# First layer's PSUM banks dealt anew: three for turned probabilities, one for all dense pieces

## What is computed

```
h = layernorm(x) * (1 + ca) + sa
x = x + ga * attn(h)          # 16 heads of 16, causal, with ALiBi, softmax over keys, then @ o_w
h = layernorm(x) * (1 + cb) + sb
x = x + gb * ffn(h)           # sigmoid(xr @ Wr) * (relu(xk @ Wk)**2 @ Wv), xr and xk mixed with the token before
```

## Time and profile before

| | us |
|---|---|
| median of 3 runs (lowest to highest) | 3240.66 (3238.57 to 3241.61) |
| the profiled execution | 3246.79 |
| its span, first to last instruction | 3245.0 |
| first layer: first transposes to last addition to x | 42.5 to 747.5 |
| of it slots 1 to 31 with the turns | 82.4 to 672.7 |
| drain behind the last AV | 689 to 747.5 |
| TensorE's mean granted clock over the span | 0.944 of full speed |

### The profile page before, as it was taken

The page is one execution under the profiler, slowest core; times in us unless marked ns, Lnnn a source line. Parts: engine busy times, 40 slices in busy tenths (PEclk is TensorE's granted clock), DMA queues, the critical chain, the costliest instruction groups (busy, mean ns, idle before and its releaser), DMA issues. The chain is left out here.

```text
span 3245.0 us, 52986 instructions
## 1 busy us (share of the span) xinstructions
PE 2931.1 (90%) x20772; PEld 1994.1 (61%) x20772; DVE 1657.6 (51%) x5057; ACT 1369.5 (42%) x2997; POOL 856.0 (26%) x830
## 2 busy tenths in 40 slices
PE   5889899975999999999999999999999688879993
PEld 2566666653575757666666666666565343668882
DVE  2566777644555544444444444455554576541114
ACT  2666666632444444445454535353433211112222
POOL 1001111122333332322323233233332100115554
PEclk8999999997999999999999999999999898669996
DMA  4110011004000000000000000100000000202325
GB/s 134 18 18 18 18 18 18 14 3 160 8 4 9 6 17 28 1 1 1 16 29 1 1 1 12 32 6 6 11 6 6 10 1 1 91 24 79 73 85 176
DMA packets 65135, 93.94 MB, mean 29 GB/s; under 512 B 9931, under 2 KB 52942, under 8 KB 63848
## 3 DMA queue, kind: packets, MB, share of 16 engines
q1 hardware_dynamic: 57208, 74.24, 7.9%
q0 software_dynamic: 7680, 16.32, 2.0%
HBM read 59.31 MB, written 27.36 MB: 27 GB/s over the span
## 5 line engine op out<-in xcount | busy, mean ns | idle before, releaser
L1371 PE MATMUL bank<-h2T,w 128*128 128x512 f32 x1024 | 479.4, 606 | 5.1 <-ACT gT L1309 3.7
L1409 PE MATMUL bank<-w,gT 128*128 128x256 f32 x2048 | 465.9, 381 | 0.0
L1409 PEld LDWEIGHTS bank<-w,gT 128*128 128x128 f32 x2048 | 379.3, 190 | 49.7 <-issue 0.5
L1046 POOL TENSOR_TENSOR prob<-prob,rsum 128x512 f32<-128x512 f32 (+1 forms) x256 | 238.1, 951 | 589.9 <-DVE rsum L1193 589.9
L1371 PEld LDWEIGHTS bank<-h2T,w 128*128 128x128 f32 x1024 | 182.4, 190 | 224.1 <-issue 173.9
L1309 ACT ACTIVATE gT<-bank,vec 128x512 f32<-128x512 f32 x256 | 175.1, 687 | 286.0 <-PE bank L1371 284.6
L633 ACT ACTIVATE y<-y,least 128x128 f32<-128x128 f32 (+3 forms) x512 | 251.9, 554 | 50.3 <-DVE least L520 50.2
L520 DVE CUSTOM_DVE_ANT_0 y<-bank,mask 128x128 f32<-128x128 f32 (+3 forms) x512 | 223.9, 486 | 77.0 <-PE bank L726 75.5
L1199 DVE COPY probT<-bank 128x1024 f32<-128x1024 f32 (+1 forms) x128 | 139.2, 1087 | 227.4 <-PE bank L1425 227.4
L1170 DVE CUSTOM_DVE_ANT_0 prob<-bank,mask 128x256 f32<-128x256 f32 (+1 forms) x512 | 164.3, 387 | 167.3 <-PE bank L1361 167.3
L1281 ACT ACTIVATE prob<-prob,least 128x256 f32<-128x256 f32 (+1 forms) x512 | 239.6, 471 | 15.8 <-DVE least L1170 15.4
(11 more groups left out here) (291 smaller groups left out, 5074.9 us busy)
## 6 DMA issues: line engine op xcount, KB each, us to landing
w<-in_W SPq DMA_DIRECT2D x8, 1024.0 KB, 5.5
expert_parts<-zeros SPq DMA_DIRECT2D x8, 1024.0 KB, 16.0
we<-in_we SPq DMA_DIRECT2D x16, 512.0 KB
rows<-modulation SPq DMA_DIRECT2D x40, 128.0 KB, 3.0
x<-in_x SPq DMA_DIRECT2D x8, 512.0 KB, 9.8
prob<-score SPq DMA_DIRECT2D x64, 64.0 KB, 2.4
probT<-score SPq DMA_DIRECT2D x64, 64.0 KB, 2.4
y<-expert_parts SPq DMA_DIRECT2D x8, 512.0 KB, 8.8
```

What stands on the lines that cost most here:

```text
L1046: nc.gpsimd.tensor_tensor(two, two, rsum[:, at:at + 2].unsqueeze(2).to_broadcast([P, 2, width]), ALU.mult).then_inc(s["probs"], 1)
L1371: ins = nc.tensor.matmul(M[m % 2][:, :], w1[:, k, m * P:(m + 1) * P], h2T[:, k, :], start=(k == 0), stop=(k == KD - 1))
L1409: ins = nc.tensor.matmul(M[i][:, (t % 2) * D:(t % 2 + 1) * D], gT[:, m, t * P:(t + 1) * P], w2[:, m, :], start=(m == 0), stop=(m == MF - 1))
```

## The change

`H` gets a third bank (4, 5, 6), and turn number `at` takes bank at % 3, with one semaphore for each bank; a turn waits until the turn three before it is emptied. `M` is bank 7 alone: a dense piece k waits until piece k-1 is emptied. The two pairs of semaphores of the dense pieces stay and still alternate, only `free` waits for k-1. `values` waits for the last three turns rather than the last two. Nothing is computed in another way, and neither the order of any queue nor the engine of any copy changes.

```diff
         def bank_of(x):
-            return M[ORDER0[x] % 2]
+            return M
...
         def free(eng, x):
-            k = ORDER0[x]
-            if k >= 2:
-                eng.wait_ge(s[("misc_out0", "misc_out1")[k % 2]], k // 2)
+            k = ORDER0[x] - 1
+            if k >= 0:
+                eng.wait_ge(s[("misc_out0", "misc_out1")[k % 2]], k // 2 + 1)
...
         def turned_out(eng, k):
-            eng.wait_ge(s[("pt_out0", "pt_out1")[k % 2]], k // 2 + 1)
+            eng.wait_ge(s[("pt_out0", "pt_out1", "pt_out2")[k % 3]], k // 3 + 1)
...
             copy(probT[:, j:j + nj, FROM[tile]:FROM[tile] + width],
-                 H[at % 2][:, 0:nj * width].rearrange("p (j n) -> p j n", j=nj))\
-                .then_inc(s[("pt_out0", "pt_out1")[at % 2]], 1)
+                 H[at % 3][:, 0:nj * width].rearrange("p (j n) -> p j n", j=nj))\
+                .then_inc(s[("pt_out0", "pt_out1", "pt_out2")[at % 3]], 1)
...
-                    if at >= 2:
-                        turned_out(pe, at - 2)
+                    if at >= 3:
+                        turned_out(pe, at - 3)
...
             def values(m, bank):
                 b, q = divmod(m, QUADS)
-                turned_out(pe, PTS * (m + 1) - 2)
-                turned_out(pe, PTS * (m + 1) - 1)
+                for k in range(3):
+                    turned_out(pe, PTS * (m + 1) - 3 + k)
```

More of the change, by code:

```diff
@@ L56 @@
         "misc_full0 misc_full1 misc_out0 misc_out1 fixed_ready fixed_placed heads_placed least0 pt_full0 "
-        "pt_out0 pt_out1 p_steps0 v_steps0 stats0 rstd0 norm0 exped0 scores_full statsf rstdf normf gated0 "
+        "pt_out0 pt_out1 pt_out2 p_steps0 v_steps0 stats0 rstd0 norm0 exped0 scores_full statsf rstdf normf gated0 "
         "ga_loaded0 ga_loaded1 gb_loaded0 gb_loaded1 stats_x rstd_x modulated rows_loaded0 rows_loaded1").split()
@@ L342, in layer0 @@
         S = c.bank[:, 0:4, :]
-        H = [c.bank[:, 4, :], c.bank[:, 5, :]]
-        M = [c.bank[:, 6, :], c.bank[:, 7, :]]
+        H = [c.bank[:, 4 + i, :] for i in range(3)]
+        M = c.bank[:, 7, :]
         L = c.loaded
         def bank_of(x):
-            return M[ORDER0[x] % 2]
+            return M
         def full(eng, x):
@@ L741, in turn_probs @@
                             src = FROM[tile] + P * key
-                            ins = nc.tensor.transpose(H[at % 2][:, col:col + P], prob[:, j0 + j, src:src + P],
+                            ins = nc.tensor.transpose(H[at % 3][:, col:col + P], prob[:, j0 + j, src:src + P],
                                                       c.ident[:, :])
```

## The result

The change made the kernel slower: median 3312.49 us (3309.62 to 3316.02, 4 runs) against 3241.14 (3238.57 to 3246.97, 4 runs), ratio 1.0218, 95% interval 1.0200 to 1.0237. The forecast was 3289 with a range of 3266 to 3318: right way, inside the range, 23.5 us too low. The profiled execution took 3309.62 us, 62.8 more than the one before; that is the difference that the views can divide.

A forecast was written before the change was run, and what follows sets the result against it. The prediction took TensorE's in-order queue in the first layer as the bound. Waits net of turn gains (+37 us, drain's 12.8 included) plus clock (+11) made 48 us, giving 3289 us against the median, range 3266 to 3318.

The forecast's parts named there:

- The bound: First layer: TensorE's in-order queue limits the time, with about 9% of holes.
- both mechanisms: First layer: a third bank removes turn waits (at most 47.4 us); each dense piece now waits for the one before.
- the boundaries of the steady batches: Dense pieces next to each other in the queue: 10.1 us of new waits per full batch, net 5.7 us slower.
- T8's gain: Turn 8 starts 1.1 us earlier where S2, a dense piece and AV follow; 0 in slots with none.
- The 6.62 us chain: S1, minima, exponentials, T10 and its copy before AV: 6.62 us in an otherwise empty slot, where T8's gain ends.
- The clock: Stalls near turns and AV halve TensorE's granted clock: +11 us, 6.5 for slot 1's AV, 5 for AV behind OUT1.
- Rival (d): The clock hardly moves: 37 us slower, 3278 us; chance 0.2.
- rival (c): The clock falls in most slots: 37 + 35 = 72 us slower, 3313 us; chance 0.2.
- the drain's: Layer's end, 690 to 747 us: dense pieces with nothing between them cost +12.8 us, with nothing charged for the clock.
- The sum: Whole kernel: 37 us of waits net of gains plus 11 us of clock, 48 us slower.
- The signs: Turn waits under 20 us, over 80 us ahead of dense pieces, batch 83 us, drain +13, layer clock below 0.96.
- Rival (a): Freed turn waits win if dense-piece emptying is covered: about 10 us faster, 3231 us; chance 0.04.

The follow-up runs named there:

- experiment 4: Changed kernel plus idle transposes behind each of the drain's 24 dense pieces, 12 behind OUT and VF, 5 behind the others: 3305.06 us.
- experiment 8: Kernel before the change, with OUT and VF freeing their bank after the first of VectorE's two operations, the product: 3242.09 us.
- experiment 2: Changed kernel plus 14 unread identity transposes between OT2 and OT3 in slot 1 of batches 1 to 7: 3300.33 us.
- experiment 1: Changed kernel with the third turn bank taken away, leaving two turn banks and one dense bank: 3338.81 us.

## Why the prediction came out as it did

- **The bound** (TensorE's queue) and both mechanisms were right, and the boundaries of the steady batches were right in size. Slot by slot at full clock, the changed kernel or its filled form costs 2.16, 0.64, 2.38 and 0.48 us over before, 5.66 a full batch against 5.7, and batch 6 costs 3.84 against 3.9. Batches 1 and 2 cost more than the 0.2 and 3.3 summed, about 2.1 and 4.3 us by my estimate (slots at full clock, in part from the traces of experiments 4 and 8). That the last AV of experiment 2 is at +24.24 where the terms had 24.5 is in part luck, since clock is in that difference as well.
- **T8's gain** was right in slots 2 and 3 (1.1 to 1.2 us) and too high in slot 0 (0.6 in batch 3). All turns together gave 26.3 us (experiment 1), near the bound of 27 for T8 alone. The 6.62 us chain limits it where little else stands in the slot, as said, and there AV waits 5 us more in all for T10's copy.
- **The clock** in the steady part: the size was right, the places were not. The forecast had 1.6 us for AV in slot 1 of four more batches and 5 us for the AV behind OUT1. All seven of the latter took 2.39 us. Slot 1 lost up to 3.0 us instead: it took 24.99, 25.33, 25.44 and 23.94 us in batches 3 to 6, and takes 22.41 at full clock. The kernel before had falls of its own, so the increase is the 6 to 12 us of experiment 2, against +11; that the total fits is luck in part. Rival (d), no clock effect, falls with experiment 2; rival (c), a fall in most slots, too: slots 2, 3 and 0 of batch 3 ran at full clock. The Trainium skill (TensorE: Matmul & The Clock Gate, A second HAM failure mode: psum-queue depth-cycling) says that short idle times between matmul groups which cycle through PSUM banks can make the clock swing between its two levels. This case agrees in kind: filling one such idle time kept the clock of slot 1 at 0.99 or 1.00 in six of seven batches. It fell in slot 1, the opening and the drain, not at each 0.7 us hole.
- **The term that was mis-sized is the drain's**, "12.8 us" and "nothing for the drain" for the clock. It measured 26.2: about 7.8 of clock and 18.4 of boundaries (experiment 4). Up to L2 the sum had 8.5 us, and with the drain filled it is 9.4 (43.02 against 33.66 us). Behind L2 it had 4.3, and it is 9.0 (50.58 against 41.56): L2.1 and VF0 each wait 0.87, VF1 1.51, and KF1, both RF and the next VF0 0.69 each, more places than the sum had. The mixing's wait of 4.25 us did not swallow any of it, since it follows the last delayed piece and is 4.25 after the change as well. A boundary also costs more than its copy: in the opening of the changed kernel two pieces of four matmuls start 2.67 us apart at full clock (53.82 behind 51.15), where such a piece takes 1.7 to 1.8 back to back, so 0.9 rather than 0.7 to 0.8:

```profile
51.15 1.99 PE L794 MATMUL bank<-hT,wqkv 128*128 128x512 f32 x4 [0.69 <-ACT score L669]
53.82 1.99 PE L794 MATMUL bank<-hT,wqkv 128*128 128x512 f32 x4 [0.69 <-ACT score L669]
```

- **The sum**: 37 + 11 = 48 us; measured 36.45 up to the last AV (forecast 24.5 + 11) + 26.2 in the drain (forecast 12.8) = 62.65 of the profiled 62.8. The medians differ by 71.35; that execution was the fastest of its four and the one before slower than its median, so some 8 us lie between executions.
- **The signs** named beforehand came: turn waits 5.8 us (under 20), a full batch of 83 us or more, over 80 us of waits ahead of dense pieces. The drain was the smaller part of the loss, 26.2 of 62.65 us, though not by far. The granted clock told nothing: over the layer it is 0.93, but it was 0.94 before, already under the 0.96 named.
- **Rival (a)**, 3231 for the freed turn waits, falls: 41.6 us fewer turn waits, and slower.

## What to carry to other kernels

Count a bank by what has to be emptied between two fills that stand next to each other in the queue, not by the size of the waits shown today: waits for dense banks were small (8.5 us ahead of AV the largest) and became the larger side, since a second bank had been hiding some 98 us (experiment 1). Give a scarce bank only to pieces that have other work between them; moving the single piece (AV) that had a turn bank free beside it was worth 42 of 71 us. Price the drain piece by piece; an idle time there that follows the delayed work gives nothing back. And give an edit that helps to both kernels before saying which division of banks is better.

## What the runs showed of the hardware

Adding work made the kernel faster twice. 98 transposes that nobody reads took 12.2 us off: in the four slots from slot 1 of batch 3 on the granted clock rose from 0.96 to 1.00, and the 80 matmuls of AV in slot 1 took 2.39 us and not 4.50. In the drain idle transposes took 7.8 us off. The place of the filling mattered: in batch 5 the clock had fallen behind two earlier holes of 0.85 and 0.81 us, and 1.7 us of transposes later in the slot changed nothing there (25.41 us for 25.44). The other three slots of a steady batch ran at 1.00 without filling, though AV waits 0.7 to 1.5 us in each.
